# The border between the second cross-attention and the integer feed-forward layer, taken up in another order

## What is computed

```python
x = x + jnp.tanh(g_xattn[1]) * _L1_xattn_ref(_layernorm(x), ctx_4096, ...)
x = x + jnp.tanh(g_ffn[1]) * _L1_ffn_ref(_layernorm(x), ...)

# the integer layer, for inv in (inv_gate, inv_up):
xs = x * inv
scale = max(max(abs(xs), axis=-1) / 127, 1e-8)
q = clip(round(xs / scale), -127, 127)
gate, up = (q @ w.T) * scale * w_scale          # each with its own q
inter = clip(silu(gate) * up, -10, 10)
# inter * inv_inter is rounded and scaled in the same way, then
y = (q_inter @ w_down.T) * scale_inter * s_down
```

## Time and profile before

| | us |
|---|---|
| median of 3 runs | 1673.97 (1673.21 to 1674.07) |
| the profiled execution, its own time | 1676.02 |
| its span, first to last instruction | 1673.8 |
| TensorE busy | 1552.4 (93%) |
| VectorE busy | 900.1 (54%) |
| ScalarE busy | 699.6 (42%) |
| GpSimd busy | 633.3 (38%) |

### The profile page before, as it was taken

One profiled execution on the slowest core, in us unless ns is written; L12 is line 12 of the kernel. 1 busy time (PEld: TensorE's weight loads), 2 busy tenths in 40 slices (PEclk: granted clock), 3 DMA queues, 4 the chain that ended last, 5 costly groups with the idle time before them and its releaser, 6 DMA issues.

```text
span 1673.8 us, 25566 instructions
## 1 busy us (share of the span) xinstructions
PE 1552.4 (93%) x8786; PEld 1231.5 (74%) x8786; DVE 900.1 (54%) x1793; ACT 699.6 (42%) x2010; POOL 633.3 (38%) x602
## 2 busy tenths in 40 slices
PE   5897978988879999999999999899899999999998
PEld 4664766657668888888888887677677777777775
DVE  5786557858831221222222223688666766776666
ACT  4443244436435444543444344553334434333442
POOL 3543135466433231331323132334544444454430
PEclk9998999989999999999999999899999999999998
DMA  5000111011120110101001010104321212212001
GB/s 208 1 2 25 52 45 38 1 57 68 45 76 26 39 51 1 64 15 37 26 27 51 1 51 30 59 34 112 93 72 51 89 39 77 64 54 74 29 14 51
DMA packets 27885, 81.41 MB, mean 49 GB/s; under 512 B 3248, under 2 KB 11952, under 8 KB 22768
## 3 DMA queue, kind: packets, MB, share of 16 engines
q1 hardware_dynamic: 26896, 79.44, 14.4%
q10 hardware_dynamic: 864, 0.30, 0.1%
HBM read 69.25 MB, written 10.49 MB: 48 GB/s over the span
## 4 chain that ended last, share of the span: by engine, by line
PE 52%; issue 12%; DVE 4%; POOL 3%; ACT 1%; POOLq 0%; DVEq 0%; ACTq 0%
PE bank L397 32%; PE bank L1296 7%; PE bank L1284 2%; PE pair L2082 2%; PE bank L2060 2%; PE pair L1265 2%; POOL wo_low L388 1%; PE pair L397 1%; PE bank L1273 1%; POOL wq_low L1021 1%; PE bank L2068 1%; POOL probs L1030 1%; DVE probs L1914 0%; DVE out_low L1944 0%; DVE small L222 0%
## 5 line engine op out<-in xcount | busy, mean ns | idle before, releaser
L397 PE MATMUL bank<-hid_high,wq_high 128*128 128x512 f32 (+1 forms) x640 | 257.6, 402 | 1.7 <-issue 1.5
L397 PE MATMUL bank<-hid_high,wq_low 128*128 128x512 f32 (+1 forms) x640 | 239.9, 375 | 0.0
L397 PE MATMUL bank<-hid_low,wq_high 128*128 128x512 f32 (+1 forms) x640 | 238.5, 373 | 0.0
L1206 DVE SCALAR_TENSOR_TENSOR x_stream<-bank,gates,x_stream 128x512 f32<-128x512 f32 x64 | 48.1, 751 | 352.8 <-PE bank L1296 352.8
L1030 POOL TENSOR_TENSOR probs<-probs,small 128x512 f32<-128x512 f32 x64 | 67.1, 1048 | 356.9 <-DVE small L1194 356.9
L1809 ACT ACTIVATE probs<-probs,small 128x64 f32<-128x64 f32 x256 | 86.2, 338 | 135.2 <-DVE small L1933 135.2
L397 PEld LDWEIGHTS bank<-hid_high,wq_high 128*128 128x128 f32 x640 | 122.9, 192 | 25.5 <-issue 4.6
L397 PEld LDWEIGHTS bank<-hid_high,wq_low 128*128 128x128 f32 x640 | 122.7, 192 | 22.8 <-issue 0.2
L397 PEld LDWEIGHTS bank<-hid_low,wq_high 128*128 128x128 f32 x640 | 123.5, 193 | 20.3 <-issue 3.1
L1104 ACT ACTIVATE probs<-pair,small 128x128 f32<-128x128 f32 x256 | 90.5, 366 | 82.8 <-DVE small L1188 80.2
L593 POOL TENSOR_TENSOR probs<-probs,small 128x512 f32<-128x512 f32 x64 | 66.8, 1043 | 127.8 <-DVE small L773 127.6
(11 more groups left out here) (339 smaller groups left out, 4012.7 us busy)
## 6 DMA issues: line engine op xcount, KB each, us to landing
raw_q<-in_L_wq SPq DMA_DIRECT2D x18, 1024.0 KB, 4.9
raw_o<-in_L_wo SPq DMA_DIRECT2D x18, 1024.0 KB, 4.9
values<-ctx_values SPq DMA_DIRECT2D x32, 256.0 KB, 4.0
values_t<-ctx_keys SPq DMA_DIRECT2D x8, 512.0 KB, 3.3
raw_c<-in_L_wkv SPq DMA_DIRECT2D x6, 512.0 KB, 3.5
raw_o<-in_L_wkv SPq DMA_DIRECT2D x5, 512.0 KB, 4.8
x_stream<-in_x SPq DMA_DIRECT2D x8, 256.0 KB, 9.9
ctx_keys<-raw_o SPq DMA_DIRECT2D x8, 256.0 KB, 2.0
```

The lines of the kernel that those rows point to most:

```text
L397: last = k.nc.tensor.matmul(out, stationary(a, c), moving(b, c), start=n == 0, stop=n == total - 1)
L1206: nc.vector.scalar_tensor_tensor(xt, k.bank[7][:], gate, xt, ALU.mult, ALU.add).then_inc(k.x_done, 1)
```

## The change

Four things, all at this border. The context groups move later by three places: group 0 to step n = 34 behind its transposes, 1 to 4 into slots 1 to 4, 5 to 8 into slots 5 to 8, then two to a slot (9 and 10, 11 and 12, 13 and 14) in slots 9 to 11, and 15 in slot 12. On VectorE the attention's loop ends at n = 32; `update(6)`, `values(15)` and `out_low(14)` stand behind the integer layer's first `normalise`, `out_low(15)` behind `clip(0)`, and `update(7)` with the statistics in slot 2 behind `inverse(1)`. On ScalarE `out_high(15)` stands behind `round_x(0)`. On TensorE the last projection stands behind `gate_up(0)`, and GpSimd takes the reciprocal roots of tiles 6 and 7 in slot 3.

```diff
-        for n in range(N + LAG + 1):
+        for n in range(N + LAG if rms else N + LAG + 1):
...
-            if rms and n - 1 in EARLY_GROUPS:
-                g = EARLY_GROUPS[n - 1]
-                ctx_evict_scalar(k, act, g, k.bank[4 + g % 2][:])
...
-        for n in range(N + LAG + 2):
+        for n in range(N + 1 if rms else N + LAG + 2):
...
-            if d >= 5 and d % 4 == 1 and not (rms and d // 4 == T):
+            if d >= 5 and d % 4 == 1 and not (rms and n == N):
...
-EARLY_GROUPS = {33: 0, 34: 1, 35: 2}
+EARLY_GROUPS = {34: 0}
...
-    INNER = {s: [s + 3] for s in range(5, 13)}
-    OUTER = {s: [s + 3] for s in range(1, 5)}
+    INNER = {s: [s] for s in range(5, 9)} | {9: [9, 10], 10: [11, 12], 11: [13, 14], 12: [15]}
+    OUTER = {s: [s] for s in range(1, 5)}
...
-            if s == 2:
+            if s == 3:
                 last_rstd_gpsimd(k, pool)
...
+        def last_values():
+            dve.wait_ge(k.vt_psum, k.at("vt_psum", 0))
+            dve.wait_ge(k.o_psum, k.at("o_psum", -2))
+            V.tensor_tensor(k.vj[:, P:2 * P], k.bank[6][:, 256:384], k.vmask[:], ALU.mult).then_inc(k.vbd_ready, 1)
+
+        def last_out_low(b, cols):
+            dve.wait_ge(k.o_hi, k.at("o_hi", b + 1 - B))
+            V.tensor_tensor(OUT[1][:, :, cols], LAST_OUT, OUT[0][:, :, cols], ALU.subtract).then_inc(k.o_lo, 1)
...
+            if s == 0:
+                last_update(T - 2)
+                last_values()
+                last_out_low(B - 2, FROM)
+            if s == 2:
+                last_update(T - 1)
+                dve.wait_ge(k.x_done, k.at("x_done", 0))
+                last_stats_vector(k, dve)
             if s == 1:
-                last_update()
-                last_stats_vector(k, dve)
...
             if 1 <= s <= T:
                 clip(s - 1)
+            if s == 1:
+                last_out_low(B - 1, TO)
...
-        ctx_product_tensor(k, pe, 3, k.bank[5][:])
+        def last_project():
+            pe.wait_ge(k.o_lo, k.at("o_lo", 0))
+            pe.wait_ge(k.x_done, k.at("x_done", -1))
...
             if s <= T:
                 gate_up(s - 1)
+            if s == 1:
+                last_project()
```

More of the change, by code:

```diff
@@ L878, in _ @@
                 queries(0, t // 2 - 1)
-        for n in range(N + LAG + 2):
+        for n in range(N + LAG + 1 if rms else N + LAG + 2):
             d = n - LAG
@@ L2390, in quant_mlp @@
     RAW = [k.kt[:, 1024:2048], k.pt[:, 1024:2048]]
-    INNER = {s: [s + 3] for s in range(5, 13)}
-    OUTER = {s: [s + 3] for s in range(1, 5)}
+    INNER = {s: [s] for s in range(5, 9)} | {9: [9, 10], 10: [11, 12], 11: [13, 14], 12: [15]}
+    OUTER = {s: [s] for s in range(1, 5)}
+    OUT = [o[:].rearrange("p (r n) -> p r n", r=4) for o in k.o]
+    LAST_OUT = k.bank[6][:, 0:256].rearrange("p (r n) -> p r n", r=4)
+    FROM, TO = slice(2 * S, 3 * S), slice(3 * S, 4 * S)
     sc = [k.small[:, 176 + 8 * i:184 + 8 * i] for i in range(4)]
@@ L2403, in _ @@
             sp.dma_start(dst, a[name + src].partition_broadcast(P)).then_inc(k.loaded_const, 16)
-        ctx_store(k, sp, 0)
         sp.wait_ge(k.o_psum, k.at("o_psum", 0))
         ctx_fetch(k, sp, 1, RAW)
-        ctx_store(k, sp, 1)
         fetch_ahead(k, sp, NEXT["F1"], "q", k.lo_q, k.at("lo_q", 0))
-        for g in range(2, CTX_GROUPS):
+        for g in range(CTX_GROUPS):
             ctx_store(k, sp, g)
@@ L2507, in exp, with last_out_high @@
             nc.scalar.activation(HB[t % 2], HB[t % 2], ACT.Identity, bias=one).then_inc(k.exp_done, 1)
-        ctx_evict_scalar(k, act, 2, k.bank[4][:])
+        def last_out_high():
+            act.wait_ge(k.o_psum, k.at("o_psum", 0))
+            nc.scalar.copy(OUT[0][:, :, TO], LAST_OUT).then_inc(k.o_hi, 1)
         for s in range(1, SLOTS):
@@ L2522, in _ @@
                 round_x(s - 1)
-            for g in OUTER.get(s - 1, [3] if s == 1 else []):
+            for g in OUTER.get(s - 1, [0] if s == 1 else []):
                 ctx_evict_scalar(k, act, g, k.bank[4 + g % 2][:])
+            if s == 1:
+                last_out_high()
             if s <= T:
@@ L2715, in down @@
             last.then_inc(k.y_psum, 1)
-        ctx_product_tensor(k, pe, 3, k.bank[5][:])
+        def last_project():
+            pe.wait_ge(k.o_lo, k.at("o_lo", 0))
+            pe.wait_ge(k.x_done, k.at("x_done", -1))
+            product(k, k.bank[7][:], lambda p, r: OUT[p][:, r, P:2 * P], lambda m, r: k.wo[m][:, r * D:(r + 1) * D],
+                    4).then_inc(k.y_psum, 1)
         for s in range(1, SLOTS):
```

7 lines of the change are left out of this document (3 added, 4 removed).

## The result

Twelve runs of the changed kernel, beside twelve of the kernel before, gave a median of 1675.18 us against 1672.59. The measured ratio is 1.0022 with an interval of 1.0013 to 1.0030, which is 2.2 to 5.0 us slower, 3.7 in the middle; the two medians alone are 2.6 apart, within that interval. The forecast was 1678.9 against 1673.97, +4.9, with 1675.0 to 1682.0 as its range, and slower by more than 0.2% at 0.71. The direction is right and the size is 1.2 us too large. Two things are less clear than that. The interval stands on both sides of 0.2%, so whether the kernel is slower by more than that is not settled. And the time of 1675.18 is only just inside the range, since the kernel before ran 1.4 us faster in these runs than in the three of the forecast; as a difference, +3.7 lies well inside +1.0 to +8.0.

The account below looks back on a forecast made before the run. TensorE, busy 93% of the span, was taken to bound the kernel through its idle time. Terms -4.3 (border lead), +8.2 (groups in slots 9 to 11) and +1.0 (clock) gave +4.9, so 1678.9 us, range 1675.0 to 1682.0.

Parts of the forecast that it names:

- What bounds the kernel: Whole layer: TensorE is busy 93% of the span; with no matmul added or removed, only its idle time matters.
- The first tile: Border: the integer chain starts sooner, so tile 0's transposes start at 370.1 in place of 380.71, 10.6 us earlier.
- The second tile: Border: VectorE and ScalarE wait for the last projection, so tile 1's transposes start at 382.5; lead shrinks to 4.3 us.
- The signs: Changed timeline: L2701 near 370 and 382.5, VectorE idle some 5 us, scaled_y 2.7 us more apart, layer 4 to 5 later.
- Slots 3 to 8: Middle of the layer: same lists, one group to a slot, so the 4.3 us lead is carried through unchanged.
- Slots 9 to 11: End of the layer: one more group each between transposes_inner and down, none hidden, 3 x 2.72 = 8.2 us lost.
- The clock: Border: TensorE's gaps grow to 2.4 and 3.8 us; lower clock behind the longer slows tile 1's transposes, 1.0 us added.
- The rival with both gaps slow: Border: the clock falls in the first gap too, costing 1.6 us on top; +6.5, 1680.5 us; chance 0.15.
- the rival with the kept clock: Border: clock kept or its loss hidden, scale(0) perhaps not waiting for GpSimd; 1677.0 to 1677.9 us; chance 0.22.
- The sum: Whole kernel: -4.3 lead, +8.2 groups, +1.0 clock, together +4.9 us.
- the band of the forecast: Whole kernel: a slowdown of +3.4 to +6 us, given chance 0.45.

Follow-up runs that it names:

- the groups alone: Kernel before with only the change's group tables, every other list in its old order; 1.0040, +6.7 us against before.
- the reordering alone: Changed kernel with context groups back at the border and slots 5 to 12 as before; 0.9972, -4.7 us against before.
- in the middle slots: Changed kernel with the doubled groups in slots 5, 6 and 7 instead of 9, 10 and 11; 1.0025, +4.2 us against before.
- the projection first: Changed kernel with the last projection right behind tile 0's transposes, ahead of group 1 and gate_up(0); 1.0000 against before.
- VectorE's wait moved: Changed kernel with only update(7) and its statistics moved behind clip(1) on VectorE; 1.0019, +3.2 us against before.
- the two best kernels: Changed kernel with projection first, groups 1, 4, 6 at the border, slots 5 to 12 as before: 0.9959; also groups of slots 9 to 11 behind down: 0.9941.

## Why the prediction was right, point by point

**What bounds the kernel.** Right: no matmul was added, and the layer is to be read by TensorE's idle time. Its pauses of more than 0.2 us, from behind `attend(15)` to the end of the layer, add up to 14.3 us before and 18.6 after, 4.3 more, where I had 4.1. That the trace has +2.75 all the same is the clock: three slow stretches before (at 395, 423 and 450 us), two after (at 379 and 444).

**The first tile.** I had it 10.6 us earlier; it was 11.6. The step that was off is `scale(0)`: it took 0.17 us at 363.83 and did not wait until the end of `smooth(1)` at 365.05. What it runs into is below.

**The second tile.** The steps were right: the end of the projection, `update(7)` with its statistics on one side, split and rounding on the other, both done within 0.6 us of each other, 3.90 us of idle time against 3.8. The lead was 5.4 against 4.3, and the whole difference is tile 0's earlier start: from its transposes to those of tile 1 it is 12.41 us, where I had 12.4. Two errors cancel in that. `clip(1)` took 0.68 and not 1.21; but `update(7)` with its statistics took 3.13 and not 2.67, because their last operation took 0.69 where it took 0.17 before. It, and not `clip(1)`, was the one beside GpSimd's split, which was through at 378.27. That the delay came out the same was foreseen in size and not in place.

**The signs.** They were given on the clock of the profile before. Read so, 2.53 us later than the changed kernel's own, the first L2701 is at 369.1 and the second at 381.5, near the 370 and 382.5 of the forecast and behind its limit of 380; on the trace's own clock the second, 378.95, would be ahead of that limit. I should have given the limit from `update(6)`. VectorE was idle for 6.15 us and not some 5. The layer ended 2.75 us later and not 4 to 5: this sign was missed.

**Slots 3 to 8.** Carried as I said, -4.86 at tile 2 and -5.41 at tile 7; the 0.5 is a slow stretch of the clock that the trace before has at 423 us and the one after has not. I had not costed this. The stretch in the kernel before:

```profile
423.00:427.00 4.00, 4.00 (x21) 3.86 (x20) 3.70 (x7) 1.79 (x5) 3.02 (x3) 0.59 0.46 85
```

**Slots 9 to 11.** The term of 8.2 us measured 2.72, 2.70 and 2.74, 8.16 in all. It is the step that the whole sign rests on, and the experiments with the groups alone, with the reordering alone and in the middle slots bear it out.

**The clock.** It fell behind the longer gap, as forecast: the eight transposes took 1.61 us and the granted clock of 379 to 383 us was 0.57. It cost 0.5 us up to tile 2 (5.37 less 4.86), half of my 1.0, since it fell only after the transposes had begun. This trace has the mildest case: in the four experiments with a pause of 3.8 to 3.9 us ahead of tile 1 the eight took 1.75 to 1.97 us, which is 0.7 to 0.9 more than at the full clock. The rival with both gaps slow did not come: the first gap was 1.31 us, not 2.4, as tile 0 was ready 1.0 us sooner than I had it, and no slow stretch followed. Of the rival with the kept clock one half came true, that `scale(0)` does not wait.

**The sum.** +4.9 forecast, +2.75 in the trace, +3.7 in the runs: 1.1 us of the difference is the lead at tile 1, 0.5 the clock, 0.5 the slow stretch that the earlier trace has. The +3.7 of the runs lies in the band of the forecast and in that of the kept clock (+2.5 to +3.9) as well, so the time does not tell them apart; the trace does, by the clock that fell. What I could have added is that a gap of 3.8 us between a projection and the tile behind it is one that a group fits into; reading my own sum by idle time shows the better kernel.

## What to carry to other kernels

When work that nothing waits for (here the context groups) is moved to let a chain start sooner, ask at its new place who waits for the instruction behind it: in a closed chain that passes through that engine it costs its full length each time, whatever the engine's share of busy time says. Filler belongs into a gap that the timeline shows, and behind the instruction that the others wait for rather than ahead of it; there it still costs what the pauses of the engine can't hold. And where two engines wait for the same result, remove both waits or bring the result forward; removing one gave next to nothing here.

## What the runs showed of the hardware

**VectorE beside GpSimd.** `scale` is an operation on two numbers a row and takes 0.17 us. Before, it took 1.00, from 375.87 to 376.87, as GpSimd was in the last of four operations, 375.66 to 376.85 (a quarter of 4.75 us each, rows 4). After, it began at 363.83, when the first of GpSimd's two operations had some 0.07 us to go (362.75 and half of 2.30), and ended at 364.00 with the second already due. So what it waits for is the one GpSimd operation that is under way, not the run of them. The last operation of the statistics in the changed kernel fits: it began at 377.61 and ended at 378.30, with the second half of GpSimd's split (375.78 and 2.49, so 378.27). Not every operation of VectorE waits: `greatest(0)` ran at its 1.21 us beside GpSimd, and `inverse(0)` took 0.17 at 364.04 with GpSimd's second operation under way. The Trainium skill, "SBUF — State Buffer", section "SBUF: two separate sides", has the pair of ports that the two engines share as an exclusive lock that the operation which starts first keeps for the whole instruction, where VectorE's operation is in a two-port mode or has two inputs in SBUF; by that rule the wait ends with one instruction, and these rows agree. Which mode VectorE's operations ran in is in no trace, and no run here isolates it.

**TensorE's clock.** In every trace with a gap of 3.8 us or more ahead of an integer tile (3.90, 3.83, 3.89, 4.45, 6.11) the transposes behind it took 1.37 to 1.97 us in place of 1.09. Behind 1.23 to 1.82 us ahead of such a tile they did not. In between it goes either way. Of four gaps of 1.95 to 1.97 us, the one with the projection first was followed by transposes of 1.76 us and that with VectorE's wait moved by 1.26; in the kernel before the clock fell when they were through, at 395 us, and with the groups alone it did not fall. Behind the 2.54 us of slot 10 it fell in eight of ten traces. And behind the 1.35 us that TensorE waits for the integers ahead of `gate_up` it mostly holds, but fell in four (before at 423 us, projection first at 419, the two best kernels at 413). In these stretches the granted clock is 0.50, the lower of the two levels, for most of their length. One cost 1.6 us where it lay in the chain of slot 10 and 0.5 to 0.8 at tile 1 of the changed kernel and three of its variants, where the wait ahead of tile 2 took the rest, so a difference between two single traces is no better than 1 to 2 us here.
